# Last tokens of all batches projected once at the start, three equal context parts per batch, queries in high and low halves

## The reference

```python
x = x + xattn(layernorm(x), ctx)        # x (8, 64, 512), ctx (8, 1601, 512), 16 heads of 32
x = x + attn(layernorm(x))              # 8 query heads, one key/value head, causal
x = x + ffn(layernorm(x))               # 2 shared experts + 8 routed experts, top 2, hidden 2048
# xattn
q, k, v = query @ Wq.T + bq, ctx @ Wk.T + bk, ctx @ Wv.T + bv
s = q k^T / sqrt(32);  a = where(s >= 0, s + 1, 1 / (1 - s));  a = a / a.sum(-1)
context = a v;  return context @ Wo.T + bo
```

## Time and profile before

| | before |
|---|---|
| median of three runs | 1272.34 us |
| profiled execution | 1272.52 us |
| its span (first to last instruction) | 1270.8 us |
| TensorE busy | 1260.8 us (99%) |
| VectorE busy | 649.4 us (51%) |
| ScalarE busy | 634.2 us (50%) |
| GpSimd busy | 437.4 us (34%) |
| moved by DMA | 174.89 MB |

### The profile page before, as it was taken

One profiled execution on the slowest core, in us unless ns is written; L12 is line 12 of the kernel. 1 busy time (PEld: TensorE's weight loads), 2 busy tenths in 40 slices (PEclk: granted clock), 3 DMA queues, 4 the chain that ended last, 5 costly groups with the idle time before them and its releaser, 6 DMA issues.

```text
span 1270.8 us, 29915 instructions
## 1 busy us (share of the span) xinstructions
PE 1260.8 (99%) x13126; PEld 1097.3 (86%) x13126; DVE 649.4 (51%) x936; ACT 634.2 (50%) x1085; POOL 437.4 (34%) x203
## 2 busy tenths in 40 slices
PE   9999999999999999999999999999999999999998
PEld 8888888888788888888789789798989999999997
DVE  5333453444463363463354454766776555565655
ACT  4445454464545544545444646646544443554443
POOL 1445345544555545545546535200032000100000
PEclk9999999999999999999999999999999999999999
DMA  6131011021011012012012111764556499999990
GB/s 244 50 103 51 18 56 50 23 68 67 19 64 68 18 56 101 19 64 68 18 51 105 51 56 43 284 255 157 179 195 224 148 348 365 340 344 347 357 396 35
DMA packets 32775, 174.89 MB, mean 138 GB/s; under 512 B 5944, under 2 KB 8152, under 8 KB 14464
## 3 DMA queue, kind: packets, MB, share of 16 engines
q1 hardware_dynamic: 30896, 168.16, 36.0%
q0 software_dynamic: 1744, 4.76, 1.2%
HBM read 166.84 MB, written 6.06 MB: 136 GB/s over the span
## 4 chain that ended last, share of the span: by engine, by line
PE 98%; DVE 1%; DMA 0%; ACT 0%; issue 0%; DVEq 0%; SPq 0%
PE bank L740 23%; PE bank L728 22%; PE bank L1079 11%; PE sc L1096 9%; PE sc L756 8%; PE sc L941 7%; PE bank L769 4%; PE sc L960 3%; PE bank L960 3%; PE bank L833 1%; PE bank L796 1%; PE bank L887 1%; PE bank L898 1%; PE sc L898 1%; DMA ctxt<-in_ctx 0%; PE sc L999 0%
## 5 line engine op out<-in xcount | busy, mean ns | idle before, releaser
L587 POOL TENSOR_TENSOR xn<-xn,tt 128x1024 f32<-128x1024 f32 x96 | 230.1, 2397 | 330.9 <-DVE tt L1325 329.7
L1208 ACT ACTIVATE tt<-sc 128x512 f32<-128x512 f32 (+1 forms) x208 | 107.8, 602 | 351.5 <-PE sc L756 351.4
L1423 DVE TENSOR_TENSOR wsl<-ring,wsh 128x2048 fp32r<-128x2048 f32 x72 | 166.8, 2316 | 111.0 <-ACT wsh L1163 107.9
L1312 DVE TENSOR_SCALAR kk<-bank,bkt 128x512 f32<-128x512 f32 (+2 forms) x130 | 80.8, 622 | 213.6 <-PE bank L728 213.2
L728 PE MATMUL bank<-cxh,wkh 128*128 128x512 f32 (+2 forms) x512 | 181.1, 354 | 1.5 <-DVE va L1320 1.0
L728 PE MATMUL bank<-cxl,wkh 128*128 128x512 f32 (+2 forms) x512 | 174.6, 341 | 0.0
L728 PE MATMUL bank<-cxh,wkl 128*128 128x512 f32 (+2 forms) x512 | 174.1, 340 | 0.0
L740 PE MATMUL bank<-wvh,cxh 128*128 128x512 f32 (+1 forms) x416 | 163.5, 393 | 0.0
L740 PE MATMUL bank<-wvl,cxh 128*128 128x512 f32 (+1 forms) x416 | 162.7, 391 | 0.0
L740 PE MATMUL bank<-wvh,cxl 128*128 128x512 f32 (+1 forms) x416 | 162.2, 390 | 0.0
L1163 ACT CAST wsh<-ring 128x2048 fp32r<-128x2048 f32 x72 | 137.4, 1909 | 48.0 <-PE sc L1096 20.9
(11 more groups left out here) (270 smaller groups left out, 2024.2 us busy)
## 6 DMA issues: line engine op xcount, KB each, us to landing
ring<-in_w SPq DMA_DIRECT2D x112, 1024.0 KB, 6.1
ctxt<-in_ctx SPq DMA_DIRECT2D x15, 1024.0 KB, 4.9
ctxt<-in_ctx SPq DMA_DIRECT2D x8, 642.0 KB, 3.9
ctxt<-in_ctx SPq DMA_DIRECT2D x10, 512.0 KB, 3.6
wqt<-in_wo SPq DMA_DIRECT2D x4, 1024.0 KB, 4.8
wqt<-in_aq SPq DMA_DIRECT2D x4, 1024.0 KB, 5.3
wqt<-in_ap_ SPq DMA_DIRECT2D x4, 1024.0 KB, 6.9
yrows<-K SPq DMA_DIRECT2D x1, 2048.0 KB, 9.1
```

What stands on the lines that cost most here:

```text
L587: e.tensor_tensor(dacc[0:kn, y, :], dacc[0:kn, y, :], tt[0:kn, w, :], ALU.add).then_inc(s["da_pool"], 1)
L1423: e.tensor_tensor(wsl[m % 3][:], ring[slot(unit_split(m))][:], wsh[m % 3][:].bitcast(F32), ALU.subtract).then_inc(s["wl_dve"], 1)
```

## The change

- Parts: each batch has three parts of 512 tokens, 24 parts in all. `key_groups` gives one group of keys to each of four slots of a part; slot 8 of a batch has none. `values_in` gives none for the last chunk.
- The last 65 tokens of the eight batches (520 tokens) are loaded together as `tails` into `ctxt`, in two halves, split, and their keys (`tail_keys`, 2 x 48 matmuls of 260 columns) and values (`tail_values`, four chunks of 128 tokens, two batches each, and one of 8 with every batch's last token) are formed before anything else. They are stored to DRAM, `ktail` and `vtail`, and in each batch loaded by `load_tail` into `ktb` (two buffers) and `va`. The scores of chunk 12 read `ktb` and wait on `kt_in`, its weighted sum waits on `vt_in`.
- Queries: rows and query weights are split in high and low halves (`xTh`, `xTl`, `woh`, `wol`), 4 x 12 matmuls of 512 columns.
- At the start weights and x are loaded in halves with semaphores of their own; part 0 is now split by ScalarE and GpSimd like the others, so `cl_pool` counts one more, and the keys of part 0 are formed after the queries.
- Buffers: `WID` is 520; some small pads between the feed-forward weights' buffers; two of them change places; the scratch for GpSimd's dynamic DMAs is set to 4096.

```diff
-SPANS = ((0, 512), (512, 512), (1024, 256), (1280, 321))
-WID = 512
+WID = 520
+TAIL = 65
-NPART = len(PARTS)
+NPART = 3 * NB
 def first(i):
-    b, (k0, n) = PARTS[i]
-    return PER * b + k0 // P
+    return PER * (i // 3) + 4 * (i % 3)
 def key_groups(slot):
+    groups = []
     for i in range(1, NPART):
+        f = first(i - 1) + ((i - 1) % 3 == 2)
+        groups += [(i, slot - f)] * (0 <= slot - f < 4)
+    return groups
 def values_in(slot):
     if slot + 2 < NCH - 3:
-        return slot + 2
-    return slot if NCH - 3 <= slot < NCH else None
+        return None if is_tail(slot + 2) else slot + 2
+    return slot if NCH - 3 <= slot < NCH - 1 else None
...
         def sync(e):
+            for h in range(2):
+                c = slice(2 * h, 2 * h + 2)
+                e.dma_start(wkt[:, c, :], wk[:, c, :]).then_inc(wk_in[h], 16)
+                e.dma_start(tail_raw[:, c, :], tails[:, c, :]).then_inc(tails_in[h], 16)
...
+            e.wait_ge(s["tl_dve"], 3)
             load_ctx(0)
...
+            def load_tail(b):
+                if b >= 2:
+                    e.wait_ge(s["s_pe"], PER * (b - 1))
+                e.dma_start(ktb[:, b % 2, :, :].rearrange("p g n -> p (g n)"),
+                            ktail[:, 4 * TAIL * b:4 * TAIL * (b + 1)]).then_inc(s["kt_in"], 16)
+                n = PER * b + PER - 1
+                e.wait_ge(s["p_pe"], n - VR + 1)
+                e.dma_start(va[0:TAIL, n % VR, :], vtail[b]).then_inc(s["vt_in"], 16)
+            e.wait_ge(s["kt_dve"], 16)
+            e.dma_start(ktail, kts.rearrange("p b g n -> p (b g n)")).then_inc(s["kt_out"], 16)
+            store_values(0)
+            store_values(1)
+            e.wait_ge(s["cl_pool"], 1)
             load_ctx(1)
+            for j in range(2, 5):
+                store_values(j)
+            e.wait_ge(s["cl_pool"], 2)
             load_ctx(2)
...
             for n in range(NCH):
                 for i in range(3, NPART):
                     if first(i - 2) - 2 == n:
-                        e.wait_ge(s["cl_pool"], i - 1)
+                        e.wait_ge(s["cl_pool"], i)
                         load_ctx(i)
+                if n % PER == PER - 2:
+                    load_tail(n // PER)
...
         def pool(e):
+            for h in range(2):
+                query_weights_lo(h)
+            context_lo(0)
             context_lo(1)
...
         def pe(e):
             def scores(n):
+                if is_tail(n):
+                    e.wait_ge(s["kt_in"], 16 * (b + 1))
                 for g in range(4):
                     for h in range(4):
+                        key = ktb[r, b % 2, g, :] if is_tail(n) else kk[r, i % 2, g, k * P:k * P + P]
+                        m = e.matmul(sc[0:kn, h, c0 + 64 * g:c0 + 64 * g + 64], key, qc[r, g, 64 * b:64 * b + 64],
+                                     start=True, stop=True)
             def weighted(n):
+                if tail:
+                    e.wait_ge(s["vt_in"], 16 * (b + 1))
...
             warm(60, bank[7])
-            first_keys()
+            tail_keys()
+            tail_values(0)
+            tail_values(1)
             for t in range(2):
                 turn(t, bank[2 + t])
+            tail_values(2)
             for t in range(2, 4):
                 turn(t, bank[t])
+            tail_values(3)
+            tail_values(4)
+            e.wait_ge(s["xt_dve"], 4)
             for g in range(4):
-                queries(g, 1)
+                queries(g)
+            for g in range(4):
+                keys(0, g)
             for n in range(2):
                 values(n)
...
         def act(e):
+            for h in range(2):
+                e.wait_ge(wq_in[h], 16)
+                e.copy(woh[:, c, :], wqt[:, c, :]).then_inc(s["wqh_act"], 1)
             context_hi(0)
+            for t in range(4):
+                turned_hi(t, bank[2 + t % 2])
             context_hi(1)
...
         def vector(e):
             def values(n):
+                if n == 0:
+                    e.wait_ge(s["vt_out"], 144)
```

More of the change, by code:

```diff
@@ L45, in first, with is_tail, tokens, place @@
 def first(i):
-    b, (k0, n) = PARTS[i]
-    return PER * b + k0 // P
[L51 to L63, removed]
+    return PER * (i // 3) + 4 * (i % 3)
+def is_tail(n):
+    return n % PER == PER - 1
+def tokens(n):
+    return TAIL if is_tail(n) else P
+def place(n):
+    b, j = divmod(n, PER)
+    return 3 * b + j // 4, j % 4
+def formed(n):
+    return (PER - 1) * (n // PER) + n % PER
 def key_groups(slot):
-    early, late = [], []
+    groups = []
     for i in range(1, NPART):
[L70 to L79, removed]
+        f = first(i - 1) + ((i - 1) % 3 == 2)
+        groups += [(i, slot - f)] * (0 <= slot - f < 4)
+    return groups
 def ending(slot, lag):
@@ L161, in projections @@
 def projections():
-    uses = [("k", 0, g) for g in range(4)] + [("v", 0), ("v", 1)]
+    uses = [("vt", j) for j in range(5)] + [("k", 0, g) for g in range(4)] + [("v", 0), ("v", 1)]
     for n in range(NSLOT):
-        early, late = key_groups(n)
         for d, what in STEPS:
@@ L171, in projections @@
         uses += [("d", b) for b in finished(n)[0]]
-        uses += [("k", i, g) for i, g in early + late]
+        uses += [("k", i, g) for i, g in key_groups(n)]
         if values_in(n) is not None:
@@ L196, in build @@
         xn = sb("xn", [P, 4, D])
+        with ExitStack() as over:
+            xTh = over.enter_context(nc.sbuf_tensor("xTh", [P, 4, D], F32R))
         with ExitStack() as over:
@@ L281, in build @@
         qc = sb1("qc", [P, 4, D])
+        with ExitStack() as over:
+            over.enter_context(nc.sbuf_tensor("tt01", [P, 2, 1024], F32))
+            xTl = over.enter_context(nc.sbuf_tensor("xTl", [P, 4, D], F32R))
         tt = sb1("tt", [P, TR, 1024])
@@ L575, in sums @@
             def sums(n):
-                kn, w, y = chunk(n)[2], n % TR, (n // PER) % 2
+                kn, w, y = tokens(n), n % TR, (n // PER) % 2
                 e.wait_ge(s["f_dve"], 2 * n + 2)
@@ L695, in take, with tail_keys @@
                 return pj[u % 2]
-            def first_keys():
-                n = width(0)
-                for h in range(2):
-                    for x_, (a, b) in enumerate(((0, 0), (1, 0), (0, 1))):
[L702 to L710, removed]
-                        for g in range(4):
[L712 to L717, removed]
+            def tail_keys():
+                for c in range(4):
+                    if c % 2 == 0:
+                        e.wait_ge(s["wkh_act"], c // 2 + 1)
+                        e.wait_ge(s["th_act"], c // 2 + 1)
+                    for x_, (a, b) in enumerate(((0, 0), (1, 0), (0, 1))):
+                        if c % 2 == 0 and x_ == 1:
+                            e.wait_ge(s["wkl_dve"], c // 2 + 1)
+                        elif c % 2 == 0 and x_ == 2:
+                            e.wait_ge(s["tl_dve"], c // 2 + 1)
+                        for g in range(4):
+                            m = e.matmul(bank[4 + g][:, 0:260], (wkh, wkl)[a][:, c, g * P:(g + 1) * P],
+                                         (cxh, cxl)[b][:, 1, c, 0:260], start=(x_ == 0 and c == 0),
+                                         stop=(x_ == 2 and c == 3))
+                            if (c, x_) == (3, 2):
+                                m.then_inc(s["ka_pe"], 1)
+                for g in range(4):
+                    for c in range(4):
+                        for x_, (a, b) in enumerate(three):
+                            m = e.matmul(bank[g][:, 0:260], (wkh, wkl)[a][:, c, g * P:(g + 1) * P],
+                                         (cxh, cxl)[b][:, 1, c, 260:520], start=(c == 0 and x_ == 0),
+                                         stop=(c == 3 and x_ == 2))
+                    m.then_inc(s["kb_pe"], 1)
@@ new lines, in tail_values @@
+            def tail_values(j):
+                dst, kn = take("vt", j), (8 if j == 4 else P)
+                col = 260 * (j // 2) + P * (j % 2)
+                if j < 2:
+                    e.wait_ge(s["kt_dve"], 8 + 2 * j + 2)
+                if j == 4:
+                    e.wait_ge(s["tl_dve"], 3)
+                for c in range(4):
+                    if j == 0 and c % 2 == 0:
+                        e.wait_ge(s["wvl_dve"], c // 2 + 1)
+                    for x_, (a, b) in enumerate(three):
+                        m = e.matmul(dst[0:kn, :], (ceh, cel)[a][:, c, :] if j == 4 else
+                                     (cxh, cxl)[a][:, 1, c, col:col + P], (wvh, wvl)[b][:, c, :],
+                                     start=(c == 0 and x_ == 0), stop=(c == 3 and x_ == 2))
+                m.then_inc(s["vt_pe"], 1)
@@ L744, in scores @@
             def scores(n):
-                i, k, kn = chunk(n)
-                u, b, c0 = i % 2, n // PER, 256 * (n - group_of(n)[0])
+                i, k = place(n)
+                b, c0, kn = n // PER, 256 * (n - group_of(n)[0]), tokens(n)
                 if n >= 2:
@@ L801, in turn @@
```

(36 more changed lines are left out.)

265 lines of the change are left out of this document (153 added, 112 removed).

## The result

The changed kernel takes 1378.09 us (median of four runs, 1377.36 to 1380.04) against 1272.32: the ratio is 1.0834, with a 95% interval of 1.0815 to 1.0853. The forecast was 1359 us with a range of 1338 to 1375: the way and the place were right, the size was 19 us short, and the time lies 3 us outside of the range. The profiled execution has a span of 1375.9 us.

What follows compares the result with a forecast made beforehand. TensorE was taken to bound the kernel, busy 1260.8 of 1270.8 us. From 1272.5: -15.8 work removed, +0.7 start, +8.3 end, +76.4 waits, +17 clock gave 1359 us, range 1338 to 1375.

Steps and rivals of the forecast that it cites:

- Work removed: TensorE's values, keys and queries: fewer or larger matmuls save 8.2, 4.7 and 2.9 us, together -15.8 us.
- one matmul of 512 columns, 0.227 us: Distance between large TensorE matmuls, read from the earlier trace as 2.72/12 and used to price the removed work.
- The sign that was named: TensorE's own sum without the slow stretches should be some 16 us smaller.
- The start: Before the first score: 54.6 us of TensorE work and 1.7 us of gaps instead of 1.0, so +0.7 us.
- The wait for the tail keys: Before chunk 12's scores, TensorE waits for a DMA queued behind a context load: 4 x 11.3 + 3 x 10.4 = 76.4 us.
- the prediction's estimate of a landing near 20: Tail keys loading beside the context load, at about 2.0 us fixed cost, would land near 20; whole some 19 us less.
- The clock in these stalls: After each of seven stalls TensorE restarts at the lower clock, 2.4 us each: 17 us.
- The warm-up: At the kernel's start TensorE runs at about half rate from 1.14 to 6.0 us, costing 2.4 us.
- The end: Attention's last slots lose keys and values, so TensorE waits 6.1 us and 2.2 us for VectorE: +8.3 us.
- That the clock would not fall: Rival: the clock does not fall in the stalls before chunk 12's scores, giving 1342 us; chance 0.22.
- that the tail keys would come in time: Rival: SP reaches the tail load well before TensorE reaches chunk 12, giving 1265.7 us, faster; chance 0.07.
- the dear reload: Rival: tail keys in 1040-byte rows land as late as a 6.9 us load, 2 to 3 us more per batch, 1380 us; chance 0.05.

Runs made afterwards that it cites:

- Experiment 6: Experiment 1's kernel with gaps so large matmuls' operands start at the same place modulo 2048 bytes, context rows 2048 bytes: 1273.56 us; with 2080-byte rows: 1281.64 us.
- experiment 1: Changed kernel with the load of a batch's tail keys and values put ahead of the same slot's context load in SP's program: 1284.65 us.
- experiment 2: Changed kernel with 190 small bf16 matmuls run on TensorE before each wait for tail keys in batches 0 to 6: 1368.42 us.
- experiment 5: Kernel before the change with 128 unused bytes behind each of four split attention weight buffers and four feed-forward buffers: 1278.30 us.
- experiment 3: Attention and feed-forward buffers moved 32 bytes further: in the kernel before the change 1272.51 us, in experiment 1's kernel 1284.10 us.
- experiment 4: Scratch for dynamic DMAs at its default in experiment 1's kernel: 1283.96 us; set to 4096 in the kernel before the change: 1272.34 us.

## Why the prediction was wrong in size

- **Work removed, -15.8 us.** It was worked out with the distances of the earlier trace rows for kernels whose buffers lie elsewhere. The counts are right. The step that failed is the one that took "one matmul of 512 columns, 0.227 us" over unchanged: with rows of 2080 bytes and the new distances it is 0.231 to 0.233, in the attention and in the feed-forward part. Experiment 6 gives the price, 11.1 us. This is the largest part of the miss, and the sum had no term for `WID` and the pads. The sign that was named, TensorE's own sum some 16 us smaller without the slow stretches, doesn't come either: its busy time rose by 14.4 us (1260.8 to 1275.2), and -15.8, 13.4 and 4.3 for the clock (below) and 11.1 make 13.0.
- **The start, +0.7.** First scores at 63.56 us; 7.5 + 54.6 + 1.7 = 63.8 was the forecast. Right, with some luck: the first matmul starts at 8.16 us and not at 7.51, as its load and ScalarE's copy end later, and from there to the first scores it is 55.4 us, not 56.3.
- **The wait for the tail keys, 76.4 us.** 80.1 measured, 11.4 a batch for 11.3 and 10.4. The mechanism and its chain are shown by the rows above and experiment 1. From the scores of chunks 10 and 11 to the late ones it is 22.9 to 23.3 us in four batches, and 23.9 to 24.1 in the three with a self-attention step, all for 22.7. In those three GpSimd's split ends at 18.5 in place of 17.4, because VectorE works on the self-attention step before it forms chunk 11's weights; I had let only TensorE's arrival move there. The DMA lands 4.8 to 5.4 us after its own issue, always with a large load in front of it in the queue. The 2.0 us behind the prediction's estimate of a landing near 20 is measured, in the Trainium skill (DMA: Bandwidth & Descriptors, "Anatomy of one DMA — SWDGE (gpsimd) path"), on DMAs that GpSimd issues; these are issued by SP. The estimate isn't borne out, and the load in front is the likely reason: the tail values of experiment 1, 130 KB too but in longer rows, are issued alone at 133.92, and nothing moves any more from 136.0 on, 2.1 us later. The tail keys alone in the queue were not tried.
- **The clock in these stalls, 17 us.** 13.4 by the seven stretches of experiment 2. The warm-up had given 2.4 us for one start; a stall cost 1.9, since the clock rose again sooner, in two of the seven batches within 3 us of resumed work.
- **The end, +8.3 us.** The waits are 6.2 and 2.2 us, where 6.1 and 2.2 were worked out. But both drop the clock too, and that I had priced only for the seven stalls. The changed kernel's chain behind the first:

```profile
886.74 3.69 PE sc L830 x64
890.42 1.86 PE bank L846 x64
892.29 5.82 PE bank L811 x24
...
905.82 1.01 PE bank L846 x32
906.82 4.19 PE sc L1025 x24
```

  Against 1.94, 1.03, 5.58, 0.64 and 3.07 at full rate these are 4.3 us more.
- **Short waits for VectorE.** Its normalisation of a finished batch fills some 8 us of a slot pair that has become shorter; TensorE waits for value copies behind it, 3.0 us in nine places where the trace of before has 1.0 in three. Not in the sum. These waits were not taken away on their own.

Corrected with measured terms: 1272.5 - 15.8 + 0.7 + 80.1 + 13.4 + 8.4 + 4.3 + 11.1 + 2.0 = 1376.7 us, against a profiled execution of 1377.7. That the clock would not fall (0.22) and that the tail keys would come in time (0.07) are refuted by the clock column and by the seven waits; the dear reload (0.05) has the time nearest to the measured one, 1380, but the wrong cause: it lands 5.0 us after its issue, not 6.9.

## What to carry to other kernels

Where one engine issues all loads in a fixed order, a new load inherits every wait of what stands before it: ask for each DMA that is added not when it is needed but when its queue gets there, and put it ahead of those that wait for something later. A stall of the engine that bounds can cost more than its length: here 11.4 us of waiting cost 1.9 us more, because the work behind it began at the lower clock. And when a buffer's row or place changes, measure the distance between two large matmuls again before counting them: the same instruction need not keep its duration.

## What the runs showed of the hardware that was not expected

In these kernels matmuls of 512 columns with 4-byte operands of the reduced format come every 0.227 us when all their operand buffers start at the same place modulo 2048 bytes (in rows of 2048 bytes), and every 0.231 to 0.233 us in the changed kernel's layout: 32 bytes a row are enough (experiment 6, 8.1 us for the kernel), and 128 bytes between buffers have an effect as well (experiment 5, 6.0 us). Moving all these buffers together by 32 bytes changes nothing (experiment 3), nor does 12288 (experiment 4), but that is six times 2048 and so no shift modulo 2048. The plain fp32 matmuls of 128 columns stay at 14.29 us for 128. Whether it is the distance between the two operands of one matmul or between those of one matmul and the next, which distances are good beside the equal ones, and what in the memory or the array they meet, was not tried.
